# Turning the attention probabilities before they are split, with transfers between SBUF rows that complete the stacked operand

## The chip, the cores and the metric

One NeuronCore of a Trainium2 chip runs the whole program. It has five instruction streams of its own: TensorE (PE; its weight loads are shown as PEld), VectorE (DVE), ScalarE (ACT), GpSimd (POOL) and SyncE (SP). They wait for each other by semaphores only. SP and POOL mostly issue DMA transfers, and 16 DMA engines carry them. The metric is the device time of one execution in microseconds, the median of repeated runs.

## The reference

Sixteen batches of 512 rows by 512 columns go through an attention block against 77 context rows each, and then through a feed-forward block. Cut to what matters:

```
enc = layernorm(x);  dec = ctx                                  # 512 x 512 and 77 x 512, 16 batches
Sim = (enc @ w1)[:, :, None] + (dec @ w2)[:, None, :] + (enc * w3) @ dec^T + b_sim     # 512 x 77
A   = softmax(Sim over the 77);  hq_hat = A @ dec               # 512 x 512
hc  = sum_i softmax(max_j Sim)[i] * enc[i]                      # one row for each batch
x   = x + concat(enc, hq_hat, enc*hq_hat, enc*hc) @ W_qv + b_qv
h   = layernorm(x) @ W1 + b1                                    # 512 -> 2048
q   = h + phase * w_imag * sin(theta + 0.1 h) * 0.1
out = x + relu(q) @ W2 + b2                                     # 2048 -> 512
```

## The kernel before

Every large product is made with split operands. A float32 value v is written as v_hi (v rounded to float32r, the type TensorE reads in one pass) and v_lo = v - v_hi. A product is then three matmuls, hi*hi, hi*lo and lo*hi, in helper `three` (L533 to L539). Where the contraction is only over the 77 context rows, two matmuls do the work of three: helper `stacked` (L541 to L546) puts parts on top of each other along the 128 partitions. The stacked operand `at_s` has two halves. Half 0 holds the 77 rows of A^T (high part) and below them rows 0 to 50 of its low part. Half 1 holds the 77 high rows again and below them rows 51 to 76 of the low part, so it has 103 rows. JA is 51 and JB is 103.

The loop `body` runs over 16 feed-forward tiles f = 0 to 15 for batch b, and in the same loop the attention of the next batch n = b + 1 is prepared, piece by piece. So the attention of batch 0 stands alone in an opening (`attention_first`, roughly the first 90 us), and attentions 1 to 15 are woven into bodies 0 to 14. The order on each engine is written out by hand with tests on f (NA is 10). For the probabilities of batch n the stages are:

- f = 5: `row_exponentials` (ACT, L922), `max_exponentials` (ACT, L926) and `probabilities` (DVE, L1251 to L1257) leave the normalised probabilities in `prob`, 128 partitions by 4 row tiles by 77.
- f = 6: `prob_high` (ACT, L932 and L933) writes their high part twice to `split_prob`, a view of the buffer `prs`; `prob_low` (DVE, two instructions of L1084) writes the low parts beside it.
- f = 8: `prob_turn` (PE, L680 and L681) turns the split copy with eight transposes into both banks of the PSUM tile `mis`, after the hidden product of tile 8. `second_stack_out` (DVE, L1273) copies half 1 to `at_s`; `stack_out` (ACT, L938, at f = 9) copies half 0.
- f = 9: `hq_hat(n, 0)` (PE, L543 and L544) is the first reader of `at_s`. The rest of the attention's products follow at f = 10.

In the first body (b = 0) the weights are also split once and stored. For it SP loads raw tiles of W1 and W2 (L439, L431), ACT and DVE split them (L892, L884 and L1084) and POOL stores them (L1606, L1612). Later bodies load the stored tiles with POOL (L1552, L1558). In the first body SP also loads the rows of batch 2 at f = 8 (`x_load`, L367). DMA issues wait in the order of the engine that issues them.

Of the kernel before, what the change touches and what calls it, by code (L numbers as in the profile page):

```python
# [37 lines left out]
P = 128  # L38
# [12 lines left out]
def xattn_ffn(nc, x, ctx_rows, w_sim, b_sim, W_qv, b_qv, W1, b1, theta, w_real, w_imag, W2, b2, x_turned, out):  # L51
# [14 lines left out]
    NA = 10  # L66
# [21 lines left out]
    with ExitStack() as ctx:  # L88
# [6 lines left out]
        def sem(name):  # L95
            return ctx.enter_context(nc.semaphore(name))
# [34 lines left out]
        at_s = sb("at_s", [P, 2, R], F32R)  # L131
        assert 2 * J + JB == 4 * J - JA
        split_prob = prs[:].rearrange("p a b r -> p (a b r)")[:, 0:RT * (2 * J + JB)].rearrange(
            "p (t k) -> p t k", t=RT)

        split_high = [split_prob[:, :, 2 * k * J:(2 * k + 1) * J] for k in range(2)]
        e_bc = sb("e_bc", [P, R])
# [71 lines left out]
        ebc_done = sem("ebc_done"); erec_done = sem("erec_done"); at_done = sem("at_done")  # L209
        split_hi = sem("split_hi"); split_lo = sem("split_lo"); at_out = sem("at_out")  # L210
        hqh_done = sem("hqh_done"); full_done = sem("full_done")
# [149 lines left out]
        def _(sp):  # L361
# [47 lines left out]
            def ctx_load(n):  # L409
# [15 lines left out]
                stack_load(n, hqw_raw, hqw_tail, hqw_dram, ctx_in)  # L425

            def raw_tile_load(p):

                need(sp, w_lo, count_of(0, p) - 1)
                src = tile_source(p, False, w2_dram, [wqv_dram[2, :, c] for c in range(C)])  # L430
                sp.dma_start(w_raw[:, p % 2], src).then_inc(w_raw_in[p % 2], 16)  # L431
# [62 lines left out]
            def body(b, par, first, last):  # L494
                n, pn = b + 1, 1 - par
                for f in range(FT):
# [10 lines left out]
                    if last:  # L507
                        continue
                    if n + 1 == B:
                        continue  # L510
# [21 lines left out]
        def _(pe):  # L532
# [142 lines left out]
            def prob_turn(n):  # L675
                pe.wait_ge(split_lo, 2 * (n + 1))
                pe.wait_ge(ebc_done, n + 1)
                for t in range(RT):
                    rows = slice(t * P, (t + 1) * P)
                    pe.transpose(mis[:, 1, rows], split_prob[:, t, 0:P].bitcast(F32), ident[:])  # L680
                    tr = pe.transpose(mis[0:JB, 0, rows], split_prob[:, t, 2 * J:2 * J + JB].bitcast(F32), ident[:])  # L681
                tr.then_inc(at_done, 1)

            def hq_hat(n, c):
                if c == 0:
                    pe.wait_ge(at_out, 2 * (n + 1))
                    pe.wait_ge(hq_lo, 2 * (n + 1))
                if c >= 2:
                    pe.wait_ge(prt_done, C * n + c - 1)
                stacked(mis[:, c % 2], lambda k, a: hqs[0:k, a, c * P:(c + 1) * P], lambda k, a: at_s[0:k, a],  # L690
                        True, True, hqh_done)
# [75 lines left out]
            def body(b, par, first, last):  # L767
                n, pn = b + 1, 1 - par
                for f in range(FT):
# [4 lines left out]
                    if f == 5 and not last:  # L774
                        spread_max(n)
                    if f == 8 and not last:
                        prob_turn(n)
# [38 lines left out]
        def _(sc):  # L816
# [111 lines left out]

            def prob_high(n):

                sc.wait_ge(prob_done, n + 1)
                nc.scalar.copy(split_high[0], prob[:]).then_inc(split_hi, 1)  # L932
                nc.scalar.copy(split_high[1], prob[:]).then_inc(split_hi, 1)  # L933

            def stack_out(n):
                sc.wait_ge(at_done, n + 1)
                need(sc, att_done, RT * n)
                nc.scalar.copy(at_s[:, 0], mis[:, 1]).then_inc(at_out, 1)  # L938

# [16 lines left out]
            def attention_first():  # L956
# [19 lines left out]
                max_exponentials(0)  # L976
                prob_high(0)
                high_parts(5)
                stack_out(0)
                context_high(0)  # L980
                high_parts(6)
                high_parts(7)
# [26 lines left out]
            def body(b, par, first, last):  # L1009
                n, pn = b + 1, 1 - par  # L1010
                for f in range(FT):
# [4 lines left out]
                    if f == 5 and not last:  # L1016
                        row_exponentials(n)
                    if f == 6 and not last:
                        prob_high(n)
                    if f == NA - 1 and not last:  # L1020
                        stack_out(n)
                        w0_high(n, 0)
# [51 lines left out]
        def _(ve):  # L1074
# [188 lines left out]

            def prob_low(n):

                ve.wait_ge(split_hi, 2 * n + 2)
                low(split_prob[:, :, J:2 * J], prob[:], split_high[0]).then_inc(split_lo, 1)
                low(split_prob[:, :, 3 * J:2 * J + JB], prob[:, :, JA:J], split_high[0][:, :, JA:J]
                    ).then_inc(split_lo, 1)

            def second_stack_out(n):
                ve.wait_ge(at_done, n + 1)
                ve.tensor_copy(at_s[0:JB, 1], mis[0:JB, 0]).then_inc(at_out, 1)  # L1273

# [87 lines left out]
            def attention_first():  # L1362
# [28 lines left out]
                row_mean_scale(0)  # L1391
                prob_low(0)
                product_add(3)
                low_part(5)
                second_stack_out(0)
                row_mean(0)
# [39 lines left out]
            def body(b, par, first, last):  # L1436
                n, pn = b + 1, 1 - par
                for f in range(FT):
# [19 lines left out]
                    if f == NA - 2 and not last:  # L1458
                        second_stack_out(n)
                    if first and 3 <= f < 3 + CN - GAP:  # L1460
# [23 lines left out]
                    if f == 6 and not last:  # L1484
                        prob_low(n)
                        row_mean_scale(n)
                        row_mean(n, range(0, C // 2))
# [199 lines left out]
```

## Time and profile before

| | |
|---|---|
| median of 3 runs | 1985.26 us (1984.53 to 1986.4) |
| profiled execution, its own time | 1987.21 us |
| its span, first to last instruction | 1985.3 us |
| mean granted TensorE clock | 0.995 |
| PE busy | 1955.8 us, 99% |
| DVE busy | 1388.4 us, 70% |
| ACT busy | 980.0 us, 49% |
| period of one body, from any line to the same line one batch on | 119.1 us |

A group of rows gives a line of the kernel, the engine, the operation and what it writes and reads. A timeline row has start and duration in microseconds; what stands in brackets at its end is the idle time before it and what ended it. PE's rows overlap: a matmul of 512 columns is shown with 0.39 us, and the next starts 0.23 us after it, so the distance of the starts is what a matmul costs.

### The profile page before, as it was taken

Reading aid. Unit: us, or ns where it says so; the run is one execution under the profiler, and the core shown is the slowest. Engines: PE = TensorE matmul, PEld = TensorE weight load, DVE = VectorE, ACT = ScalarE, POOL = GpSimd, SP = SyncE. Lnnn points to the kernel's source line nnn. Section 1 sums busy time; section 2 is a strip of 40 time slices with the busy share of each in tenths; the row PEclk is TensorE's granted clock in tenths of the full one; section 3 lists DMA queues with packets and bytes.
Section 4 is the critical chain, followed back from the end, with each engine's and each line's share of the span. In section 5 each row is a group of like instructions: output and inputs, shape, how many; then the busy total and the mean of one; then the engine's idle time right before and its main releaser. Section 6 shows DMA issues by size and latency. Waiting matters only on the chain.

```text
span 1985.3 us, 24769 instructions
## 1 busy us (share of the span) xinstructions
PE 1955.8 (99%) x8832; PEld 1604.4 (81%) x8832; DVE 1388.4 (70%) x2406; ACT 980.0 (49%) x1654; POOL 385.5 (19%) x834
## 2 busy tenths in 40 slices
PE   6989999999999999999999999999999999999999
PEld 5777788888888888888888888888888888888887
DVE  6787776767767577676767767577676767767554
ACT  6474553635446363553635446363553635446343
POOL 0122212121121212112121121212112121121110
PEclk9999999999999999999999999999999999999999
DMA  7466947658476674748748476674748648475473
GB/s 256 153 227 233 303 148 239 216 158 242 148 220 196 195 226 145 233 148 240 216 159 242 147 221 196 193 227 145 232 148 239 217 161 239 146 223 184 140 216 122
DMA packets 142599, 394.17 MB, mean 199 GB/s; under 512 B 25655, under 2 KB 35379, under 8 KB 140556
## 3 DMA queue, kind: packets, MB, share of 16 engines
q0 software_dynamic: 83584, 304.31, 49.6%
q1 hardware_dynamic: 58748, 88.23, 14.2%
q8 instruction: 72, 1.18, 0.2%
q14 instruction: 51, 0.42, 0.1%
q10 hardware_dynamic: 144, 0.04, 0.0%
HBM read 351.68 MB, written 40.85 MB: 198 GB/s over the span
## 4 chain that ended last, share of the span: by engine, by line
PE 92%; DMA 2%; DVE 2%; ACT 1%; issue 1%; SPq 0%; ACTq 0%; POOL 0%; DVEq 0%; POOLq 0%
PE acc L535 17%; PE acc L537 17%; PE acc L536 17%; PE hid L535 12%; PE hid L537 11%; PE hid L536 11%; PE mis L636 1%; DMA w_raw<-in_L_ffn_W 1%; PE mis L543 1%; PE acc L544 1%; PE acc L543 1%; PE mis L544 1%; PE mis L537 1%; PE mis L535 1%; PE mis L536 1%
## 5 line engine op out<-in xcount | busy, mean ns | idle before, releaser
L535 PE MATMUL hid<-T,w1s 128*128 128x512 f32 x1024 | 404.9, 395 | 8.0 <-DVE w1s L1084 6.5
L535 PE MATMUL acc<-ws,act 128*128 128x512 f32 x1024 | 403.1, 394 | 0.0
L537 PE MATMUL hid<-T,w1s 128*128 128x512 f32 x1024 | 400.5, 391 | 0.0
L536 PE MATMUL hid<-T,w1s 128*128 128x512 f32 x1024 | 400.2, 391 | 0.0
L537 PE MATMUL acc<-ws,act 128*128 128x512 f32 x1024 | 399.9, 390 | 0.0
L536 PE MATMUL acc<-ws,act 128*128 128x512 f32 x1024 | 399.4, 390 | 0.0
L1224 DVE TENSOR_SCALAR kk<-ph 128x512 f32<-128x512 f32 x256 | 108.9, 425 | 353.1 <-ACT ph L899 353.1
L908 ACT ACTIVATE act<-h 128x512 fp32r<-128x512 f32 x256 | 162.0, 633 | 349.4 <-DVE h L1216 328.2
L899 ACT ACTIVATE ph<-hid,hbias 128x512 f32<-128x512 f32 x256 | 175.6, 686 | 306.3 <-PE hid L537 305.7
L1558 POOL DMA_DIRECT2D ws<-w2x_dram x240 | 127.1, 530 | 555.2 <-PE acc L537 545.7
L535 PEld LDWEIGHTS hid<-T,w1s 128*128 128x128 f32 x1024 | 193.4, 189 | 50.6 <-DVE w1s L1084 7.7
L1230 DVE SCALAR_TENSOR_TENSOR act<-h,act 128x512 fp32r<-128x512 f32 x256 | 176.1, 688 | 74.1 <-ACT act L908 72.8
L537 PEld LDWEIGHTS hid<-T,w1s 128*128 128x128 f32 x1024 | 193.1, 189 | 40.9
L537 PEld LDWEIGHTS acc<-ws,act 128*128 128x128 f32 x1024 | 192.6, 188 | 40.6
L536 PEld LDWEIGHTS hid<-T,w1s 128*128 128x128 f32 x1024 | 193.5, 189 | 38.9
L535 PEld LDWEIGHTS acc<-ws,act 128*128 128x128 f32 x1024 | 192.6, 188 | 39.3
L536 PEld LDWEIGHTS acc<-ws,act 128*128 128x128 f32 x1024 | 192.7, 188 | 38.9
L1552 POOL DMA_DIRECT2D w1s<-w1x_dram x240 | 128.9, 537 | 456.0 <-PE hid L537 444.0
L1216 DVE SCALAR_TENSOR_TENSOR h<-ph,camp,h 128x512 f32<-128x512 f32 x256 | 191.0, 746 | 0.0
L902 ACT ACTIVATE h<-hid,cols 128x512 f32<-128x512 f32 x256 | 174.2, 680 | 26.1 <-DVE act L1230 26.1
L1226 DVE TENSOR_TENSOR ph<-ph,kk 128x512 f32<-128x512 f32 x256 | 177.3, 693 | 8.8
L912 ACT ACTIVATE ph<-ph 128x512 f32<-128x512 f32 x256 | 158.3, 618 | 0.4
(181 smaller groups left out, 2739.3 us busy)
## 6 DMA issues: line engine op xcount, KB each, us to landing
w1s<-w1x_dram POOLq DMA_DIRECT2D x240, 512.0 KB, 3.8
ws<-w2x_dram POOLq DMA_DIRECT2D x240, 512.0 KB, 4.5
ws<-wqx_dram POOLq DMA_DIRECT2D x56, 512.0 KB, 3.6
full<-in_x_turned SPq DMA_DIRECT2D x15, 1024.0 KB, 8.1
out_x<-X SPq DMA_DIRECT2D x15, 1024.0 KB, 4.8
X<-in_x SPq DMA_DIRECT2D x14, 1024.0 KB, 6.7
w_raw<-in_L_ffn_W SPq DMA_DIRECT2D x32, 256.0 KB, 4.9
w1x_dram<-w1s POOLq DMA_DIRECT2D x16, 512.0 KB, 3.8
```

The costliest lines, as they stand in the source:

```text
L535: pe.matmul(dst, w_hi, m_hi, start=start, stop=False)
L536: pe.matmul(dst, w_hi, m_lo, start=False, stop=False)
L537: mm = pe.matmul(dst, w_lo, m_hi, start=False, stop=stop)
L899: nc.scalar.activation(ph[:, f % 2], hid[:, f % 2], ACT.Identity, bias=hbias[:, f:f + 1], scale=HSCALE).then_inc(t_done, 1)
L902: nc.scalar.activation(h2[:, f % 2], hid[:, f % 2], ACT.Identity, bias=b1c[:, f:f + 1], scale=1.0).then_inc(h2_done, 1)
L908: nc.scalar.activation(act[:, f % 4, 0], h2[:, f % 2], ACT.Relu).then_inc(act_hi, 1)
L912: nc.scalar.activation(ph[:, f % 2], ph[:, f % 2], ACT.Sin, scale=TWO_PI_BELOW).then_inc(s_done, 1)
L1216: ve.scalar_tensor_tensor(out=h2[:, f % 2], in0=ph[:, f % 2], scalar=camp[:, f:f + 1], in1=h2[:, f % 2], op0=ALU.mult, op1=ALU.add).then_i ...
L1226: ve.tensor_tensor(ph[:, f % 2], ph[:, f % 2], kk[:], ALU.subtract).then_inc(r_done, 1)
L1230: ve.scalar_tensor_tensor(out=act[:, f % 4, 1], in0=h2[:, f % 2], scalar=0.0, in1=act[:, f % 4, 0].bitcast(F32), op0=ALU.max, op1=ALU.subtract
L1552: po.dma_start(w1s[:, s].rearrange("p a c k -> p (a c k)"), w1x_dram[f % FT].rearrange("p a c k -> p (a c k)")).then_inc(w1_in[s], 16)
L1558: po.dma_start(ws[:, slot_of(p)], tile_source(p, last, w2x_dram, wqx_dram)).then_inc(w_in[slot_of(p)], 16)
```

## The change

The probabilities are no longer split before they are turned. PE turns `prob` itself with four transposes, at f = 7 in place of 8. ACT copies the turned 77 rows from PSUM into half 0 as their high part, and copies that from SBUF into half 1. DVE subtracts the high part from the PSUM rows and writes all 77 low rows to `at_lo`, a free piece of `prs` on partitions 0 to 76. Two DMA transfers then move the low rows to the partitions below the high ones, 51 rows of 2 KB into half 0 and 26 rows into half 1. SP issues them at f = 8, and ACT does so in the opening. `hq_hat(n, 0)` waits for both.

```
-        at_s = ...; split_prob = prs[...]; split_high = [...]
+        at_lo = prs[0:J, 1, 1]
...
+            def stack_low_in(n):                                    # SP, at f == NA - 2
+                sp.wait_ge(at_low, n + 1)
+                sp.dma_start(at_s[J:P, 0].bitcast(F32), at_lo[0:JA].bitcast(F32)).then_inc(at_in, 16)
+                sp.dma_start(at_s[J:JB, 1].bitcast(F32), at_lo[JA:J].bitcast(F32)).then_inc(at_in, 16)
...
             def prob_turn(n):
-                pe.wait_ge(split_lo, 2 * (n + 1))
-                pe.wait_ge(ebc_done, n + 1)
+                pe.wait_ge(prob_done, n + 1)
                 for t in range(RT):
-                    pe.transpose(mis[:, 1, rows], split_prob[:, t, 0:P].bitcast(F32), ident[:])
-                    tr = pe.transpose(mis[0:JB, 0, rows], split_prob[:, t, 2 * J:2 * J + JB].bitcast(F32), ident[:])
+                    tr = pe.transpose(mis[0:J, 1, t * P:(t + 1) * P], prob[:, t], ident[:])
...
             def hq_hat(n, c):
                 if c == 0:
+                    pe.wait_ge(ebc_done, n + 1)
                     pe.wait_ge(at_out, 2 * (n + 1))
+                    pe.wait_ge(at_in if n else at0_in, 32 * max(n, 1))
...
-            def prob_high(n): ...                                   # ACT, two copies, f == 6
             def stack_out(n):                                       # ACT, f == NA - 1 before, NA - 2 now
                 sc.wait_ge(at_done, n + 1)
-                nc.scalar.copy(at_s[:, 0], mis[:, 1]).then_inc(at_out, 1)
+                nc.scalar.copy(at_s[0:J, 0], mis[0:J, 1]).then_inc(at_out, 1)
+                sc.wait_ge(at_out, 2 * n + 1)
+                nc.scalar.copy(at_s[0:J, 1], at_s[0:J, 0].bitcast(F32)).then_inc(at_out, 1)
+            def first_stack_low_in(): ...                           # ACT, opening: the two transfers of batch 0
...
-            def prob_low(n): ...                                    # DVE, two subtractions, f == 6
-            def second_stack_out(n): ...                            # DVE, one copy, f == 8
+            def stack_low(n):                                       # DVE, f == 8
+                ve.wait_ge(at_out, 2 * n + 1)
+                low(at_lo, mis[0:J, 1], at_s[0:J, 0]).then_inc(at_low, 1)
```

On PE, in the first body, these rows stand between two matmul groups before the change (f = 8; the hidden product ends above, the product with W2 begins below):

```order
L680 MATMUL mis<-ident,prs 128x128 [waits ebc_done,split_lo]
L681 MATMUL mis<-ident,prs 103x128
L680 MATMUL mis<-ident,prs 128x128
L681 MATMUL mis<-ident,prs 103x128
L680 MATMUL mis<-ident,prs 128x128
L681 MATMUL mis<-ident,prs 103x128
L680 MATMUL mis<-ident,prs 128x128
L681 MATMUL mis<-ident,prs 103x128
```

And these stand there now, one tile earlier, with the matmuls on either side:

```order
L541 MATMUL hid<-T,w1s 128x512
L682 MATMUL mis<-ident,prob 77x128 [waits prob_done]
L682 MATMUL mis<-ident,prob 77x128 x3
L539 MATMUL acc<-ws,act 128x512 [waits w_lo,act_lo]
L540 MATMUL acc<-ws,act 128x512
```

Eight rows have become four, the wait is for the probabilities alone, and the place is after the hidden product of tile 7.

On SP, in the first body around f = 8, before the change (L431 loads raw tiles for the second weights, L439 those of W1, L367 the rows of batch 2):

```order
L439 DMA w_raw<-in_L_ffn_W 128x4x128 [waits w1_lo]
L431 DMA w_raw<-in_L_xattn_W_qv 128x512 [waits w_lo]
L367 DMA X<-in_x 128x4x512 [waits p_late2,p_late3,p_late1,p_late0]
L439 DMA w_raw<-in_L_ffn_W 128x4x128 [waits w1_lo]
L431 DMA w_raw<-in_L_xattn_W_qv 128x512 [waits w_lo]
```

The same place now (L426 and L427 are the new transfers, L363 and L441 the loads named before):

```order
L433 DMA w_raw<-in_L_xattn_W_qv 128x512 [waits w_lo]
L426 DMA at_s<-prs 51x512 [waits at_low]
L427 DMA at_s<-prs 26x512
L363 DMA X<-in_x 128x4x512 [waits p_late2,p_late3,p_late1,p_late0]
L441 DMA w_raw<-in_L_ffn_W 128x4x128 [waits w1_lo]
```

The load of batch 2 and the raw W1 tile now stand behind SP's wait for `at_low`.

On ACT, in the opening, before the change (L846 and L851 are the copies of the next context chunk):

```order
L938 CAST at_s<-mis 128x512 [waits at_done]
L876 CAST hqs<-ctx_raw 128x512 [waits hq0_in]
L877 CAST hqs<-ctx_raw 39x512
L876 CAST hqw<-ctx_raw 128x512 [waits hqw0_in]
L877 CAST hqw<-ctx_raw 39x512
L846 CAST act<-acc 128x504 [waits c_mm,c_tr]
```

And now:

```order
L935 CAST at_s<-mis 77x512 [waits at_done]
L937 CAST at_s<-at_s 77x512 [waits at_out]
L879 CAST hqs<-ctx_raw 128x512 [waits hq0_in]
L880 CAST hqs<-ctx_raw 39x512
L879 CAST hqw<-ctx_raw 128x512 [waits hqw0_in]
L880 CAST hqw<-ctx_raw 39x512
L942 DMA at_s<-prs 51x512 [waits at_low]
L943 DMA at_s<-prs 26x512
L849 CAST act<-acc 128x504 [waits c_mm,c_tr]
```

One copy and two DMA issues have come in ahead of the next context chunk.

## Rows read from the trace of the kernel before

**Rows 1.** The page: busy us, share of the span and instructions.
```profile
PE 1955.8 (99%) x8832; PEld 1604.4 (81%) x8832; DVE 1388.4 (70%) x2406; ACT 980.0 (49%) x1654; POOL 385.5 (19%) x834
```

**Rows 2.** Waits of PE: total us, times, longest.
```profile
PE hid L535 <- DVE w1s L1084: 6.5, 2, 3.6
...
PE mis L543 <- DVE hqw L1084: 2.7, 1, 2.7
```

**Rows 3.** Timeline of PE in a later body: start, duration.
```profile
983.49 0.39 PE L537 MATMUL hid<-T,w1s 128*128 128x512 f32 x1
983.72 0.27 PE L680 MATMUL mis<-ident,prs 128*128 128x128 f32 x1
...
984.83 0.40 PE L536 MATMUL acc<-ws,act 128*128 128x512 f32 x1
...
992.78 0.39 PE L543 MATMUL mis<-at_s,hqs 128*128 128x512 f32 x1
```

**Rows 4.** Timeline of DVE in that body.
```profile
977.41 0.65 DVE L1084 TENSOR_TENSOR prs<-prob,prs 128x308 fp32r<-128x308 f32 x2
...
980.72 0.43 DVE L1224 TENSOR_SCALAR kk<-ph 128x512 f32<-128x512 f32 x1 [0.54 <-ACT ph L899]
...
987.69 0.69 DVE L1273 CAST at_s<-mis 103x512 fp32r<-103x512 f32 x1
```

**Rows 5.** Timeline of ACT in that body.
```profile
974.27 0.44 ACT L932 CAST prs<-prob 128x308 fp32r<-128x308 f32 x1
...
974.96 0.69 ACT L899 ACTIVATE ph<-hid,hbias 128x512 f32<-128x512 f32 x1
```

**Rows 6.** Timeline of SP: a 6 KB store, the load that waits for it, a 51-row load.
```profile
1035.28 0.32 SPq L377 DMA_DIRECT2D stat_dram<-mean_bc  x1
1036.63 0.34 SPq L381 DMA_DIRECT2D mean_bc<-stat_dram  x1
...
1039.55 0.31 SPq L404 DMA_DIRECT2D ctx_raw<-in_ctx  x1
```

**Rows 7.** Windows: us, busy by engine, PEclk, share of the 16 DMA engines, GB/s.
```profile
990.00:990.50 0.50, 0.50 (x3) 0.39 (x3) 0.50 (x1) 0.25 (x1) 0.00 (x0) 1.00 1.10 410
...
1040.50:1040.75 0.25, 0.25 (x5) 0.25 (x4) 0.00 (x0) 0.25 (x1) 0.02 (x1) 1.00 0.19 59
```

**Rows 8.** The page: a kind of DMA issue, KB each, median us to landing.
```profile
w_raw<-in_L_ffn_W SPq DMA_DIRECT2D x32, 256.0 KB, 4.9
```

**Rows 9.** Timeline of POOL in that body, a weight load.
```profile
987.79 0.53 POOL L1558 DMA_DIRECT2D ws<-wqx_dram  x1 [3.08 <-PE acc L537]
```

**Rows 10.** Timeline of ACT, then DVE, then PE in the opening.
```profile
41.53 0.59 ACT L938 CAST at_s<-mis 128x512 fp32r<-128x512 f32 x1 [1.70 <-PE mis L681]
...
53.37 0.68 DVE L1084 TENSOR_TENSOR act<-acc,act 128x504 fp32r<-128x504 f32 x1 [0.51 <-ACT xin L851]
...
47.88 0.77 PE L543 MATMUL mis<-at_s,hqs 128*128 128x512 f32 x1 [2.65 <-DVE hqw L1084]
...
54.22 0.39 PE L543 MATMUL mis<-at_s,hqs 128*128 128x512 f32 x1
```

**Rows 11.** First body: SP, DVE, ACT and PE around the raw W1 tile.
```profile
147.02 0.38 SPq L367 DMA_DIRECT2D X<-in_x  x1
147.44 0.51 SPq L439 DMA_DIRECT2D w_raw<-in_L_ffn_W  x1
...
148.74 0.68 DVE L1273 CAST at_s<-mis 103x512 fp32r<-103x512 f32 x1
...
156.01 0.62 ACT L892 CAST w1s<-w_raw 128x512 fp32r<-128x512 f32 x1 [3.32 <-DMA w_raw<-in_L_ffn_W]
...
157.41 0.79 PE L535 MATMUL hid<-T,w1s 128*128 128x512 f32 x1 [2.88 <-DVE w1s L1084]
```

**Rows 12.** Windows: granted TensorE clock in the first body and after it.
```profile
157.41:163.10 5.69, 5.69 (x13) 4.46 (x14) 4.88 (x8) 1.34 (x3) 1.06 (x2) 0.50 0.84 285
...
1000.00:1900.00 900.00, 900.00 (x4088) 741.20 (x4087) 626.06 (x1073) 431.12 (x718) 179.87 (x392) 1.00 0.63 193
```

More of the change, by code:

```diff
@@ L131, in xattn_ffn @@
         at_s = sb("at_s", [P, 2, R], F32R)
[L132 to L136, printed above, removed]
+        at_lo = prs[0:J, 1, 1]
         e_bc = sb("e_bc", [P, R])
@@ L209, in xattn_ffn @@
         ebc_done = sem("ebc_done"); erec_done = sem("erec_done"); at_done = sem("at_done")
-        split_hi = sem("split_hi"); split_lo = sem("split_lo"); at_out = sem("at_out")
+        at_out = sem("at_out"); at_low = sem("at_low"); at_in = sem("at_in"); at0_in = sem("at0_in")
         hqh_done = sem("hqh_done"); full_done = sem("full_done")
@@ L508, in body @@
                         continue
+                    if f == NA - 2:
+                        stack_low_in(n)
                     if n + 1 == B:
@@ L675, in prob_turn @@
             def prob_turn(n):
-                pe.wait_ge(split_lo, 2 * (n + 1))
-                pe.wait_ge(ebc_done, n + 1)
+                pe.wait_ge(prob_done, n + 1)
                 for t in range(RT):
-                    rows = slice(t * P, (t + 1) * P)
-                    pe.transpose(mis[:, 1, rows], split_prob[:, t, 0:P].bitcast(F32), ident[:])
-                    tr = pe.transpose(mis[0:JB, 0, rows], split_prob[:, t, 2 * J:2 * J + JB].bitcast(F32), ident[:])
+                    tr = pe.transpose(mis[0:J, 1, t * P:(t + 1) * P], prob[:, t], ident[:])
                 tr.then_inc(at_done, 1)
@@ L775, in body @@
                         spread_max(n)
-                    if f == 8 and not last:
+                    if f == 7 and not last:
                         prob_turn(n)
@@ L927, in max_exponentials @@
                                      ).then_inc(ebc_done, 1)
[L929 to L933, printed above, removed]
             def stack_out(n):
@@ L937, in stack_out, with first_stack_low_in @@
                 need(sc, att_done, RT * n)
-                nc.scalar.copy(at_s[:, 0], mis[:, 1]).then_inc(at_out, 1)
+                nc.scalar.copy(at_s[0:J, 0], mis[0:J, 1]).then_inc(at_out, 1)
+                sc.wait_ge(at_out, 2 * n + 1)
+                nc.scalar.copy(at_s[0:J, 1], at_s[0:J, 0].bitcast(F32)).then_inc(at_out, 1)
+            def first_stack_low_in():
+                sc.wait_ge(at_low, 1)
+                nc.scalar.dma_start(at_s[J:P, 0].bitcast(F32), at_lo[0:JA].bitcast(F32)).then_inc(at0_in, 16)
+                nc.scalar.dma_start(at_s[J:JB, 1].bitcast(F32), at_lo[JA:J].bitcast(F32)).then_inc(at0_in, 16)
             def w0_high(n, c):
@@ L976, in attention_first @@
                 max_exponentials(0)
-                prob_high(0)
                 high_parts(5)
@@ L980, in attention_first @@
                 context_high(0)
+                first_stack_low_in()
                 high_parts(6)
@@ L1017, in body @@
                         row_exponentials(n)
-                    if f == 6 and not last:
-                        prob_high(n)
+                    if f == NA - 2 and not last:
+                        stack_out(n)
                     if f == NA - 1 and not last:
-                        stack_out(n)
                         w0_high(n, 0)
@@ L1262, in row_mean_scale @@
                 ve.reciprocal(erec[:], esum[:]).then_inc(erec_done, 1)
[L1264 to L1273, printed above, removed]
+            def stack_low(n):
+                ve.wait_ge(at_out, 2 * n + 1)
+                low(at_lo, mis[0:J, 1], at_s[0:J, 0]).then_inc(at_low, 1)
             def row_mean(n, chunks=range(C)):
@@ L1391, in attention_first @@
                 row_mean_scale(0)
-                prob_low(0)
                 product_add(3)
                 low_part(5)
-                second_stack_out(0)
+                stack_low(0)
                 row_mean(0)
@@ L1458, in body @@
                     if f == NA - 2 and not last:
-                        second_stack_out(n)
+                        stack_low(n)
                     if first and 3 <= f < 3 + CN - GAP:
@@ L1484, in body @@
                     if f == 6 and not last:
-                        prob_low(n)
                         row_mean_scale(n)
```

## The prediction

> **What bounds the kernel now.** I read the page first. PE is busy 99% of the span, DVE 70% and ACT 49% [rows 1]. The reader should see that no other engine can be the bound over the whole program. Next come PE's waits. They are few: the longest two groups are 6.5 us in two waits on a raw W1 tile and 2.7 us in one wait in the opening [rows 2]. Then PE's timeline. The last wait of more than a few tenths ends at 157.41 [rows 11], and from 1000 to 1900 PE is busy 900.00 of 900.00 us at full clock [rows 12]. So the program has two parts. In the opening and in body 0 the chain runs through ACT, DVE, SP and DMA as well as PE, and PE stalls. In bodies 1 to 14 time is what PE issues, and an instruction there that goes is a gain, as long as no new wait takes its place. Last come the timelines of DVE, ACT, SP and POOL around the places the change touches.
>
> **Transposes in bodies 1 to 14.** The eight transposes start at 983.72, and the second matmul after them starts at 984.83 [rows 3]. That is 1.11 us, less the 0.23 us of the one matmul between, so 0.88 us for eight, 0.11 us each. (The 0.27 us shown for one overlaps its neighbours; multiplying it by the count would claim too much.) The four that remain have the same 128 moving columns and fewer stationary ones, so I take 0.11 us for them too. The saving is 0.44 us in a body and 14 x 0.44 = 6.2 us. Moved to f = 7 they start about 978.3, and their only wait, for the probabilities, is long met: ACT already copies those at 974.27 [rows 5]. So the new place costs nothing.
>
> **ACT and DVE in a body.** ACT loses two copies at f = 6, 0.69 us by the distance from 974.27 to 974.96 [rows 5], and gains one of about 0.57 us, now ahead of the phase of tile 8. That phase waits for PE's hidden product anyway, which comes 0.44 us later relative to the transposes. DVE loses 0.57 us at 977.41, and has one 0.69 us instruction for another at 987.69 [rows 4]. Neither bounds a later body, so I count 0. What this does set is when the low rows are ready. DVE waited at 980.72 for ACT [rows 4], and that ACT work comes 0.69 us earlier. DVE is full from there, so the low rows start near 987.0 and end near 987.7.
>
> **The new wait in bodies 1 to 14.** `hq_hat` starts at 992.78 now [rows 3] and would start at 992.34. The transfers have 4.6 us. Their landing is not in the trace, so I bound it. A 6 KB store and the load that waits for it are issued 1.35 us apart [rows 6]; this is the fixed part under load. The 51 rows are 104 KB. In the window in which a 51-row load is likely to be alone, 0.19 of the 16 engines, about three, carry 59 GB/s [rows 6, 7], which makes 1.8 us. A weight load of 512 KB shares these engines. POOL issues it at 987.79 [rows 9], 0.44 us earlier after the change. Its 32 KB on each engine, at 410/16 = 26 GB/s [rows 7], make 1.3 us. The sum is 4.4 us, so landing is near 992.1, and the cover is 0.2 us. The low end spreads 104 KB over all engines at 410 GB/s, 0.3 us, so 1.6 us in all and a cover of 3.0. The high end is the 4.9 us in which 256 KB land behind other loads [rows 8], plus 0.35 us for the second issue: 5.3 us, a wait of 0.7 us, 9.8 us over 14 bodies. I take 0, near the middle value, knowing that the cover is thin.
>
> The window shows about three busy engines. The Trainium skill has a rule for it (DMA: Bandwidth & Descriptors, section "Why a DMA increments its semaphore by 16 and not by 1"): the number of engines is the largest one up to 16 that divides the row count. By that rule 51 rows run on 3 engines and 26 on 13, which speaks against cutting the stack at 51; the trace agrees with its 0.19. Without the rule the low end would be the likely one.
>
> Queued behind SP's wait for `at_low` there is nothing near in a later body: the rows of the next batch are loaded before it, the turned rows 25 us after it.
>
> **The opening: +0.8 us.** ACT copies the stack at 41.53, when PE's transposes end [rows 10]. With four fewer this is near 41.1. Then it makes two copies with a wait between (1.2 us) in place of one, which puts the next work 0.25 us later. Two DMA issues follow, 0.31 us each in SP's row [rows 6] and more with the gaps, 0.75 us in all. So the next context chunks come 1.0 us later, and ACT has nothing idle before the last of them: DVE waits for ACT at 53.37 [rows 10]. DVE would end this one near 55.0 in place of 54.05. PE starts its next stacked product at 54.22 [rows 10], so it would start near 55.0. The 0.44 us of the transposes vanish in the wait that ends at 47.88 [rows 10]. The transfers are issued near 44.9 and land near 48, as the wait for `hqw` ends. Bounds: 0.3 if the issues are short, 1.3 if the landing at 48 slips too.
>
> **Body 0: +1.8 us.** PE stalls 2.88 us until 157.41 for the raw W1 tile of f = 11. SP issued that load at 147.44 behind the 1 MB load at 147.02, and ACT got it at 156.01 [rows 11]. Now both stand behind `at_low`. DVE reaches that place at 148.74 [rows 11], 0.7 us sooner after the change because the f = 6 pieces are off this body's chain, so the low rows are ready near 148.7. Two issues of 0.35 us and one of 0.4 us put the raw W1 load at 149.9, 2.4 us later. The landing should move less, since the 1 MB cannot start before the tile load ahead of it is through, and one such load takes 4.9 us [rows 8]. Half of 2.4 is 1.2 us, the rows of the stack in front add up to 0.7 us. I take 1.8, between 1.2 and 2.6. The 0.44 us of the transposes are lost in this stall, and so is the wait for the stack transfers just ahead of it.
>
> **The clock: -0.5 us.** After the stall the granted clock is 0.50 for 5.69 us [rows 12], which is the 1.2 GHz level, and costs about 2.8 us. The stall of the opening has the same after it. A later restart may find a shorter slow stretch, or a longer one elsewhere. I bound this by -2.8 and +2.8 and take a small gain, because PE would restart closer to the end of the present stretch.
>
> **Sum.** -6.2 + 0.8 + 1.8 - 0.5 = -4.1 us. The profiled execution took 1987.21 us and would take 1983.1. The median is 1.95 us below that execution, 1985.26, so the prediction is 1981.2 us.
>
> **Rivals.**
> 1. *The transfers land late and PE waits in each body.* One mechanism: the transfer of 51 rows on few engines beside a weight load. From 0.29 us a body it eats the whole net gain, and at the high end of 0.7 us the time is 1981.2 + 9.8 = 1991.0, slower. For it: the cover of 0.2 us, and the 4.9 us of a loaded queue [rows 8]. Against it: the 1.35 us round trip [rows 6] and the sum of 4.4. The Trainium skill (same page, section "Latency and other measured facts") has a fixed cost of about 2 us, most of it the receipt from the target, with HBM the slowest. With it in place of 1.35 the landing would be 5.1 us and the wait 0.5; the trace's own round trip, written to HBM, is shorter.
> 2. *The early part eats the gain.* Opening 1.3, body 0 2.4, and 1.5 us more at the slow clock: -6.2 + 5.2 = -1.0, so 1984.3 us. For it: ACT and DVE are full where the pieces are added [rows 10]. Against it: it needs all three at their upper ends.
> 3. *Body 0 gets shorter.* The removed split lay on its chain, 0.69 us of ACT and 0.57 us of DVE [rows 4, 5], and the slow stretch may go. Opening 0.5, body 0 0.6, clock -2.8: -7.9, so 1977.4 us. Against it: SP's order, which does not depend on these.
>
> That the transposes are not really halved is excluded by the order of PE's instructions.
>
> **How the numbers follow.** The forecast (cover holds) has 0.52, with its own range 1978.5 to 1984; rival 1 has 0.20, rival 2 0.14, rival 3 0.14. A measurement of this kernel tells about 0.2%, 4.0 us, from no change, so the line is at 1981.3 and the forecast lies on it: 0.31 of it counts as faster and 0.21 as the same. Rival 3 and a little of rival 2 make faster 0.47. Same is 0.21 + 0.03 (a short wait of rival 1) + 0.11 = 0.35. Slower is 0.17 + 0.01 = 0.18. The range runs from below rival 3 to rival 1's full wait: 1977.0 to 1991.0.
>
> **What would show it.** PE's four transposes at a distance of 0.11 us, and a body of 118.7 us in place of 119.1. No idle time before the first `at_s` matmul in bodies 1 to 14; a wait there for `at_s` by DMA shows rival 1. In the opening the matmul of 54.22 near 55.0. In body 0 the stall before the hidden product of f = 11 ending near 160 in place of 157.41, with SP's raw W1 issue near 150. The prediction is wrong if the body is not shorter, or if the first 165 us grow by more than 4 us or shrink.

## The result and the profile after: slower by 0.6%

| | before | after |
|---|---|---|
| median | 1985.83 us (1984.53 to 1986.93, 4 runs) | 1999.39 us (1996.83 to 2000.4, 4 runs) |
| ratio | | 1.0061, 95% interval [1.0048, 1.0073] |
| span of the profiled execution | 1985.3 us | 1998.6 us |
| period of a body | 119.12 us | 119.83 us |

The prediction said 1981.2 us, and 1991.0 at most. The time went the other way and beyond the range, and the body, which was to be 118.7 us, is longer than before.

The page of the changed kernel, busy us, share and instructions (before: [rows 1]):

```profile
PE 1949.5 (98%) x8768; PEld 1594.1 (80%) x8768; DVE 1378.9 (69%) x2374; ACT 980.5 (49%) x1638; POOL 385.7 (19%) x834
```

PE has 64 instructions fewer and is busy 6.3 us less, as intended, and the span is still 13.3 us longer. So PE must wait somewhere new. Its waits (total us, times, longest; before: [rows 2]) name the place:

```profile
PE mis L547 <- DMA at_s<-prs: 17.2, 15, 4.0
...
PE hid L539 <- DMA w1s<-w1x_dram: 2.5, 1, 2.5
PE mis L640 <- DVE xin L1331: 2.2, 1, 2.2
```

Fifteen waits for the transfers, one in each body from 0 to 14. None of them was there before. PE's timeline in the body that [rows 3] shows:

```profile
985.50 0.39 PE L541 MATMUL hid<-T,w1s 128*128 128x512 f32 x1
985.72 0.60 PE L682 MATMUL mis<-ident,prob 128*77 128x128 f32 x4
986.08 0.48 PE L539 MATMUL acc<-ws,act 128*128 128x512 f32 x1
...
999.56 0.39 PE L541 MATMUL acc<-ws,act 128*128 128x512 f32 x1
1000.63 0.47 PE L547 MATMUL mis<-at_s,hqs 128*128 128x512 f32 x1 [0.68 <-DMA at_s<-prs]
1000.94 0.40 PE L548 MATMUL mis<-at_s,hqs 103*128 103x512 f32 x1
```

The four transposes take 0.44 us where eight took 0.88, counted as in the prediction: the second matmul behind them starts at 986.39, so 0.67 us less the 0.23 of one matmul. The first matmul on `at_s` was due at 999.79, 0.23 us after the one before it, and starts at 1000.63. That is 0.84 us late. The bracket says 0.68, since it counts from the shown end of a matmul that overlaps the next. In the 14 later bodies the bracket is between 0.66 and 1.22 us, 0.94 on average, which makes 1.10 us of lateness.

Windows of PE show both sides of it: between 1000 and 1900 PE was busy 900.00 us [rows 12] and now is idle for 7.5 us of the same stretch, eight waits in eight bodies:

```profile
1000.00:1900.00 900.00, 892.46 (x4032) 732.73 (x4033) 622.16 (x1059) 428.74 (x708) 177.77 (x388) 1.00 0.63 192
```

**The chain in front of that matmul.** DVE, ACT, SP and POOL in the same body (before: [rows 4 to 6], [rows 9]):

```profile
994.43 0.68 DVE L1088 TENSOR_TENSOR prs<-mis,at_s 77x512 fp32r<-77x512 f32 x1
...
990.37 0.56 ACT L935 CAST at_s<-mis 77x512 fp32r<-77x512 f32 x1
990.97 0.62 ACT L937 CAST at_s<-at_s 77x512 fp32r<-77x512 f32 x1
...
995.14 0.79 SPq L426 DMA_DIRECT2D at_s<-prs  x1
995.98 0.87 SPq L427 DMA_DIRECT2D at_s<-prs  x1
...
994.81 0.53 POOL L1553 DMA_DIRECT2D ws<-wqx_dram  x1 [2.19 <-PE acc L541]
```

The reader should see three things. DVE's input, ACT's first copy, was ready at 990.93 (990.37 + 0.56), and the subtraction started 3.5 us later, since DVE's order puts it behind the sine term of tile 8. Each issue holds SP for 0.8 us and not the 0.31 of a 51-row load from memory [rows 6]. And POOL issued 512 KB of weights 0.33 us before the first transfer. The windows after that (share of the 16 engines and GB/s are the last two columns) show what moved:

```profile
995.50:996.00 0.50, 0.50 (x4) 0.42 (x3) 0.50 (x2) 0.40 (x2) 0.00 (x0) 1.00 0.00 0
996.00:997.00 1.00, 1.00 (x6) 0.84 (x5) 0.91 (x2) 0.43 (x1) 0.00 (x0) 1.00 0.87 209
997.00:998.00 1.00, 1.00 (x7) 0.81 (x6) 0.17 (x2) 0.73 (x2) 0.47 (x1) 1.00 0.93 328
```

Two microseconds of all engines, about the 512 KB of the weight load, come first. The list of DMA packets (queue, packets, MB, share of the 16 engines; POOL's transfers go through q0, those of SP through q1) has the stack's rows apart. From 995.14 to 997.90, and then from 997.90 to 999.70:

```profile
q0 software_dynamic: 136, 0.51, 62.2%
```

```profile
q0 software_dynamic: 50, 0.17, 45.1%
q1 hardware_dynamic: 93, 0.16, 25.4%
```

All 77 rows of the stack lie in the second stretch. So the first row moves 2.76 us after the issue, the last one is through 1.79 us later, and PE starts 0.94 us after that, together 5.49 us. PE was due 4.65 us after the issue. In the 14 later bodies the first row moves 2.56 to 2.87 us after the issue, and PE starts 5.42 to 6.02 us after it, 5.74 on average.

**Body 0.** SP and then PE (before: [rows 11]):

```profile
146.74 0.83 SPq L426 DMA_DIRECT2D at_s<-prs  x1
147.62 0.84 SPq L427 DMA_DIRECT2D at_s<-prs  x1
...
149.94 0.80 SPq L441 DMA_DIRECT2D w_raw<-in_L_ffn_W  x1
...
152.11 0.77 PE L547 MATMUL mis<-at_s,hqs 128*128 128x512 f32 x1 [4.01 <-DMA at_s<-prs]
159.51 0.50 PE L539 MATMUL hid<-T,w1s 128*128 128x512 f32 x1 [1.43 <-DVE w1s L1088]
...
212.63 1.11 PE L640 MATMUL mis<-ident,xin 128*128 128x128 f32 x8 [2.15 <-DVE xin L1331]
227.65 0.50 PE L539 MATMUL hid<-T,w1s 128*128 128x512 f32 x1 [2.53 <-DMA w1s<-w1x_dram]
```

The raw W1 load goes out at 149.94 (147.44 before), and the stall behind it ends at 159.51 (157.41 before). Two later waits for what the raw tiles feed are new or longer.

Where the 13.3 us of the two profiled executions lie: up to the last wait of the opening (117.61 before, 116.61 now) the changed kernel is 1.0 us ahead. From there to the start of `hq_hat(2, 0)` in body 1 it loses 5.0 us. The 13 periods from there to body 14 cost 9.2 us, and the end 0.1.

### The profile page after: what moved, and what is told of

Read it like the earlier page. It is cut to its first block, busy times and chain, and to the rows that moved or that the text cites. A ratio compares the mean times of both kernels' runs of the same rounds, so it can differ in the third digit from the quotient of the medians.

```text
span 1998.6 us, 24625 instructions
## 1 busy us (share of the span) xinstructions
PE 1949.5 (98%) x8768; PEld 1594.1 (80%) x8768; DVE 1378.9 (69%) x2374; ACT 980.5 (49%) x1638; POOL 385.7 (19%) x834
## 3 DMA queue, kind: packets, MB, share of 16 engines
q8 instruction: 71, 1.16, 0.2%
## 4 chain that ended last, share of the span: by engine, by line
PE 72%; DVE 9%; ACT 7%; DMA 6%; issue 5%; SPq 1%; POOL 0%; ACTq 0%; DVEq 0%; POOLq 0%
PE acc L539 13%; PE acc L541 13%; PE acc L540 13%; PE hid L539 9%; PE hid L541 9%; PE hid L540 9%; DMA at_s<-prs 3%; DVE h L1220 2%; ACT L915 2%; ACT ph L902 2%; DVE kk L1228 1%; PE mis L640 1%; ACT L929 1%; DVE ph L1230 1%; DMA w_raw<-in_L_ffn_W 1%
```

## The experiments

All times are compared with the kernel before on the same chip. "Late" is the longest bracket before the first `at_s` matmul in bodies 1 to 14. "Early part" is the start of `hq_hat(2, 0)`, which stands in body 1, less the start of the last transposes that wait in the opening (117.61 before, 116.61 after). This mark itself lies between 116.4 and 118.6 us in the eleven profiles, so what comes before it is left out. The early part is that of one profile for each kernel and moves too; the ratio rests on all the timed runs.

| run | ratio and interval | period, us | late, us | early part, us |
|---|---|---|---|---|
| before | 1 | 119.12 | none | 160.45 |
| after | 1.0061 [1.0048, 1.0073] | 119.83 | 1.22 | 165.44 |
| a_no_transfers | 0.9967 [0.9955, 0.998] | 118.65 | none | 158.87 |
| b_rows_45_32 | 1.0007 [0.9998, 1.0016] | 118.86 | 1.20 | 165.15 |
| c_low_earlier | 0.9985 [0.9976, 0.9993] | 118.65 | none | 163.49 |
| d_first_body_order | 1.0068 [1.0056, 1.0081] | 119.68 | 1.16 | 163.89 |
| i_small_load_ahead | 0.9985 [0.9976, 0.9994] | 118.67 | none | 164.02 |
| e_early_51 | 0.9975 [0.9965, 0.9985] | 118.65 | none | 160.76 |
| f_early_45 | 0.9971 [0.9961, 0.9982] | 118.59 | none | 159.72 |
| g_low_earlier_45 | 0.998 [0.9971, 0.9989] | 118.59 | none | 160.09 |
| h_body0_none | 0.9971 [0.9962, 0.9979] | 118.65 | none | 162.55 |

**1. The price of the wait.** SP issues no transfer in the bodies, and PE waits for none.

```diff
-                    if f == NA - 2:
-                        stack_low_in(n)
-                    pe.wait_ge(at_in if n else at0_in, 32 * max(n, 1))
+                    pe.wait_ge(at0_in, 32)
```

> Leaves out the two transfers in bodies 0 to 14, so the low rows that stand in at_s are those of batch 0; all else is the changed kernel. Theory (the landing of the transfers costs each of the 14 later bodies 0.94 us of waiting and some 0.2 us of restart): the period falls from 119.83 to 118.68 us, PE shows no wait before the first at_s matmul, and body 0 loses SP's two issues of 0.83 us; 1999.4 - 16 - 1 to 4 = 1979 to 1983 us, below the kernel before. Rival 1 (the period is longer because of the new order of PE, ACT and DVE, and the wait only takes up slack that is there anyway): the period stays above 119.3 and the time above 1990. Rival 2 (only the early part is hurt by the transfers): period 119.8, time 1996.

Measured: 1980.17 us against 1987.48, ratio 0.9967, period 118.65. PE's timeline:

```profile
987.16 0.40 PE L539 MATMUL acc<-ws,act 128*128 128x512 f32 x1
987.40 0.39 PE L545 MATMUL mis<-at_s,hqs 128*128 128x512 f32 x1
```

No bracket: the wait is gone, and the body is 1.17 us shorter than in the changed kernel and 0.47 us shorter than before. The theory holds, and both rivals fall. 0.94 us of idle time cost 1.17: 0.16 for the overlap that the bracket leaves out, and the rest in the first matmuls behind the wait (0.31 us apart in place of 0.23). The last is argued from the rows, not tested. The 0.47 us is what the body gains by the transposes and the new order together, and 14 times it, 6.6 us, is all of this kernel's lead over the kernel before by the ratio (0.33%, 6.6 us).

**2. Fewer rows on more engines.** The cut of the low rows is moved from 51 and 26 to 45 and 32.

```diff
-    JA = P - J
+    JA = 45
```

(`P` becomes `J + JA` where half 0 is filled and multiplied.)

> The changed kernel with the stack cut at 45 and 32 low rows in place of 51 and 26 (halves of 122 and 109 rows). The Trainium skill (DMA: Bandwidth & Descriptors, section Why a DMA increments its semaphore by 16 and not by 1) has the number of engines as the largest up to 16 that divides the row count: 15 and 16 here, in place of 3 and 13. Theory A (the 51 rows on three engines are what makes the landing late; 17 rows each one after the other, the packets run 1.75 us): the packets take about 0.5 us, the wait of 0.94 us in a body goes, period 118.7, time near 1984. Theory B (the wait is the issue on SP of 0.8 us twice, and the queue behind the weight load that POOL issues 0.33 us earlier): the landing is at most 0.3 us earlier, period 119.5 or more, time 1995 to 1999.

Measured: ratio 1.0007, period 118.86, 0.96 us shorter than in the changed kernel. SP's issues take nearly as long as before (0.90 and 0.60 us, together 1.50 in place of 1.66), and the weight load is as near. SP and POOL in its timeline:

```profile
991.01 0.90 SPq L426 DMA_DIRECT2D at_s<-prs  x1
991.96 0.60 SPq L427 DMA_DIRECT2D at_s<-prs  x1
...
990.67 0.53 POOL L1553 DMA_DIRECT2D ws<-wqx_dram  x1 [2.19 <-PE acc L541]
```

From 991.01 to 993.60 only q0 moves packets. From 993.60 to 994.80:

```profile
q1 hardware_dynamic: 108, 0.16, 39.9%
```

The first row moves 2.61 us after the issue, as late as before, but the last one is through 1.05 us later, in place of 1.79. So the three engines of the 51 rows cost about 0.9 us of landing in this body (3.66 us to the end of the last row in place of 4.55) and 0.96 of the period. The Trainium skill's rule that the number of engines is the largest one up to 16 that divides the row count (DMA: Bandwidth & Descriptors, section "Why a DMA increments its semaphore by 16 and not by 1") forecasts 15 and 16 here, and this run agrees: besides the 77 rows, q1 has 31 short packets here and 16 in the changed kernel, that is 15 + 16 and 3 + 13. Three of the 14 bodies still show a wait (1.20, 0.59 and 0.24 us), and the period is 0.27 us above the 118.59 of the kernels below with the same cut and no wait, so the cover is about nothing here. Theory A's 1984 us was too low, and so was its 0.5 us for the packets. Theory B fails: the period is below its 119.5.

**3. The same transfers 2.3 us sooner.** Only the place of DVE's subtraction moves.

```diff
-                    if f == NA - 2 and not last:
-                        stack_low(n)
...
                     if f == 7 and not last:
                         row_mean(n, range(C // 2, C))
                         context_low(n)
+                        stack_low(n)
```

> The changed kernel with DVE's subtraction of the stack at the end of tile 7 instead of after the sine term of tile 8, where its input has been ready for 2.9 us. Theory (only the lateness counts): the low rows are ready 2.3 us sooner, the landing is before PE gets to the first at_s matmul, the period is 118.7 and the time 1999.4 - 16 = 1983.5 or less. Rival 1 (the transfers always run right behind the next weight load, whose issues are 2.72 us apart, so that moving them 2.3 us moves the landing by less than 1 us or not at all): period 119.4 to 119.8, time 1994 to 1999. Rival 2 (DVE has no 0.6 us to give there and the product with W2 waits for act): period above 119.3 with waits of PE for act.

Measured: ratio 0.9985, period 118.65, no wait in the later bodies. The theory holds (1984.3 us, where 1983.5 or less was expected). DVE had the 0.68 us of this instruction to give: PE shows no new wait for it. From the first issue to the matmul it is now 6.97 us. The wait in body 0 stays, 2.92 us in place of 4.01.

**4. The load ahead.** This separates the queue from the issue and the engines. The weight load issued just ahead of the transfers is cut to an eighth.

```diff
-                po.dma_start(ws[:, slot_of(p)], tile_source(p, last, w2x_dram, wqx_dram)
+                q = 16 if p == FIRST + C - 1 and not last else P
+                po.dma_start(ws[0:q, slot_of(p)], tile_source(p, last, w2x_dram, wqx_dram)[0:q]
```

> The changed kernel with one weight load of each later body cut down: the load that POOL issues 0.33 us before the two transfers of the stack (994.81 against 995.14 in the changed kernel) brings 16 partitions, 64 KB, in place of 128, 512 KB; the other 112 partitions keep older weights. Theory (the transfers start only when that load is through, 2.7 us after their issue, of which 1.8 us is the queue): they start and land 1 to 1.8 us sooner, the wait of 0.94 us before the first at_s matmul goes or falls under 0.1, period 118.65 to 118.75, ratio 0.998 to 0.999. Rival (the time goes in SP's issues of 0.8 us, the three engines and the receipt, and the load ahead has no part): the wait stays above 0.6 us, period 119.5 or more, ratio 1.004 or above.

Measured: ratio 0.9985, period 118.67, no wait above 0.1 us in the later bodies. POOL and SP, then a window:

```profile
988.89 0.51 POOL L1554 DMA_DIRECT2D ws<-wqx_dram  x1 [2.19 <-PE acc L541]
...
989.24 0.79 SPq L426 DMA_DIRECT2D at_s<-prs  x1
```

```profile
990.50:991.50 1.00, 1.00 (x6) 0.84 (x5) 0.69 (x1) 0.17 (x2) 0.00 (x0) 1.00 0.17 37
```

The packets from 989.24 to 990.66, and then from 990.66 to 992.93:

```profile
q0 software_dynamic: 40, 0.07, 23.2%
```

```profile
q1 hardware_dynamic: 93, 0.16, 23.3%
```

With nothing large ahead the first row moves 1.43 us after the issue, in place of 2.76 (1.38 to 1.44 in the 14 later bodies). At 0.17 of 16, about three engines, one sees the 51 rows alone. The last row is through 3.68 us after the issue, in place of 4.55. So the weight load ahead held the start back by 1.33 us and the landing by 0.87 of the 5.49 us (0.97 in the mean of the 14 bodies); why the rows take longer from first to last when they start sooner (2.26 us against 1.79) was not tested. The theory holds against its rival. The cover is about nothing here too: 3.68 and the 0.94 us from the last row to PE make 4.62, and PE is due at 4.65.

**5. Body 0, SP's order.** The rows of batch 2 and the raw W1 tile go first.

```diff
                             raw_w1_load(f + 2)
+                        if f == NA - 1:
+                            stack_low_in(n)
-                    if f == NA - 2:
+                    if f == NA - 2 and not first:
```

> The changed kernel with SP's order in body 0 alone changed: the load of batch 2's rows and the raw W1 tile of f = 11 first, the two transfers of the stack behind them. Theory (the early part is 4.0 us longer since these loads stand behind the transfers in SP's order): the stall before the hidden product of f = 11 ends near 157.5 again, as in the kernel before, the first at_s matmul of body 0 waits longer, and the start of hq_hat(2,0) is 2 to 4 us sooner than 282.05; time 1995.5 to 1997.5. Rival (what is longer is set by ACT and DVE behind the first at_s matmul of body 0): the early part is as long or longer, time 1999 to 2002. The period stays at 119.83 by both.

Measured: ratio 1.0068, 1999.75 us, not distinguishable from the changed kernel. Neither text had it whole: by the time the rival is right, and in the profile the early part is 1.6 us shorter. The raw W1 load did go out at 145.00, as meant. But the transfers stood behind the 1 MB load, and PE waited 8.96 us for them:

```profile
147.01 0.84 SPq L426 DMA_DIRECT2D at_s<-prs  x1
...
157.33 0.76 PE L549 MATMUL mis<-at_s,hqs 128*128 128x512 f32 x1 [8.96 <-DMA at_s<-prs]
```

154 KB took 10.3 us from issue to use. So with either order one of the two groups is late in body 0, as long as the low rows are ready only at 147.

**6. Body 0 without its two transfers,** otherwise as in 3.

```diff
-                    if f == NA - 2:
+                    if f == NA - 2 and not first:
                         stack_low_in(n)
```

> As c_low_earlier, but body 0 leaves out its two transfers, so that batch 1 is computed with the low rows of batch 0; bodies 1 to 14 have theirs. Theory (the transfers of body 0 alone cost 4.6 us there by SP's order and the wait behind them): the early part, hq_hat(2,0) less the start of body 0, falls from 163.5 to 159, time near 1980.5 where the kernel before has 1987.5, ratio 0.9965. Rival (the early part depends on chance in the opening, 1 us either way, more than on the transfers): ratio 0.998 or above.

Measured: ratio 0.9971 against 0.9985 for number 3. The difference, 0.0014 or 2.8 us, is the best estimate of what body 0's transfers cost there, though the intervals of the two just overlap. The ratio speaks for the theory (0.9965) and against the rival, whose 0.998 lies just outside the interval. But the early part of the profiled execution, 162.55, did not fall to 159 as expected. In it the raw W1 tile, issued at 147.35, reached ACT at 157.56, 10.2 us later, where it took 9.0 in a_no_transfers. One profile is not enough to size this part, so its size rests on the timed runs.

**7. All of it earlier.** The transposes at f = 6, ACT's copies and DVE's subtraction at the start of f = 7, and in body 0 the transfers between the raw W1 tile of f = 10 and the next raw tile, once with 51 rows, once with 45.

```diff
-                    if f == 7 and not last:
+                    if f == 6 and not last:
                         prob_turn(n)
-                    if f == NA - 2 and not last:          # ACT stack_out, DVE stack_low
+                    if f == NA - 3 and not last:
```

> The changed kernel with the whole chain one tile earlier: PE's four transposes at f = 6, ACT's two copies and DVE's subtraction at the start of f = 7, and in body 0 SP issues the two transfers between the raw W1 tile of f = 10 and the next raw tile, not behind that tile. Theory (in body 0 SP has nothing to do but wait for the low rows from 144.3 on, and everything it issues later pays for that): the raw W1 load of f = 11 goes out near 146 instead of 149.9, the first at_s matmul of body 0 waits under 1 us, hq_hat(2,0) starts near 277 to 279 instead of 282.05, the period is 118.65: 1981 to 1983 where the kernel before has 1987.5 (ratio 0.9965 to 0.998). Rival (the early subtraction on DVE and the copies on ACT delay the sines in body 0, which is full there, by as much as they give): hq_hat(2,0) at 281 or later, ratio 0.9985 or above.

> The same chain one tile earlier, and the stack cut at 45 and 32 rows. Theory: in later bodies nothing is left to gain, period 118.65; in body 0 the transfers are 1 us shorter, which counts only if the first at_s matmul still waits there: ratio equal to that of the same kernel with 51 rows, or up to 0.0005 below it. Rival (fewer engines per transfer leave room for the raw tile loads beside them, so that 15 and 16 engines hold those up): 0.0005 above it.

Measured: 0.9975 and 0.9971. Both lie in the range that was expected for the first (0.9965 to 0.998), and with 51 rows `hq_hat(2, 0)` starts at 277.93, as the theory had it. With 45 rows the time is 1981.2 us against 1987.48, faster than the kernel before by 0.29% and than the changed one. SP in body 0 of the kernel with 45 rows, then PE:

```profile
140.76 0.96 SPq L426 DMA_DIRECT2D at_s<-prs  x1
141.76 0.62 SPq L427 DMA_DIRECT2D at_s<-prs  x1
...
145.40 0.38 SPq L363 DMA_DIRECT2D X<-in_x  x1
145.83 0.51 SPq L441 DMA_DIRECT2D w_raw<-in_L_ffn_W  x1
...
156.39 0.80 PE L541 MATMUL hid<-T,w1s 128*128 128x512 f32 x1 [4.68 <-DVE w1s L1090]
```

The transfers now fill time in which SP had nothing to issue, the raw load is out at 145.83 in place of 149.94, and the first `at_s` matmul of body 0 has no wait. The early part is 159.72, 5.7 us shorter than in the changed kernel, of which about 1.2 is body 1's own wait. The two cuts differ by less than their intervals.

**8. The earlier subtraction and 45 rows.** The edits of 3 and 2 together.

> The subtraction at the end of tile 7 (as in the run named c_low_earlier) and the cut at 45 and 32. Theory: period 118.65 as there; in body 0 the wait of 2.9 us before the first at_s matmul becomes about 1.9, the early part is up to 1 us shorter: ratio 0.998 to 0.9985. If 0.9985 is missed on the upper side, the length of the transfers has no part in body 0.

Measured: 0.998, as expected but not distinguishable from 0.9985. The wait of body 0 is 1.26 us in place of 2.92 (1.9 was expected), and from the first issue to the matmul it is 4.59 us in place of 6.84. So the engines seem to have a part there too; it is one profile of each.

## Why the prediction was wrong

**The step that failed** is "The new wait in bodies 1 to 14": a landing of 4.4 us, a cover of 0.2 us, "I take 0". Its cover was right (4.64 us forecast, 4.68 measured from the end of the subtraction to PE's due time). The landing took 5.49 in the body shown and 5.74 on average. By the parts of the sum, in the body shown:

| part | forecast | measured |
|---|---|---|
| all that is fixed | 1.35 us | 2.37 us: 1.43 from the issue to the first row with nothing large ahead (number 4), and 0.94 from the last row to PE's matmul |
| the rows of the stack on three engines | 1.8 us | 1.79 us, first to last row |
| the weight load ahead | 1.3 us | 1.33 us later start (2.76 in place of 1.43) |
| sum | 4.4 us | 5.49 us |

The fixed part was the term that was mis-sized, by 1.0 us, and the other two were right to a tenth. (The measured parts add up by construction, since the load's part is the difference of two starts.) The forecast's 1.35 came from a 6 KB store and the load that waits for it, 1.35 us apart [rows 6], whose issue is short (0.32 us against 0.79). The Trainium skill has about 2 us (DMA: Bandwidth & Descriptors, section "Latency and other measured facts"), which I cited and set aside in favour of the trace's shorter pair. The measured 2.37, which includes PE's start, is nearer to it, though HBM, which it names as the slowest target, has no part in these transfers. That two terms came out exactly is in part luck: one was read from a window that was only likely to hold the load alone, and the weight load's 1.33 us at the start is worth only 0.87 at the landing.

It was a mistake of judgement too. A cover of 0.2 us on a sum of three bounded terms is a coin toss with 14 bodies behind it, and it got a chance of 0.52 against 0.20. Rival 1 was the mechanism, and the high end of its landing, 5.3 us, was near. Its price was low, 0.7 us a body against 1.17: the landing is later still, so PE is 1.10 us late on average, and the restart adds 0.08. So the later bodies cost 9.9 us where a gain of 6.2 was forecast, and this alone takes the time out of the range.

**The transposes** were right: 0.44 us a body forecast, 0.44 by their starts and 0.47 by the period (number 1). Moving them to f = 7 cost nothing that shows.

**The later bodies' sum.** 14 x (1.17 - 0.47) = 9.8 us longer by the price of the wait, 9.9 by the periods, 14 x (119.83 - 119.12).

**The opening** was forecast as 0.8 us longer and is not: PE starts its next stacked product at 53.09, where 54.22 was before [rows 10] and 55.0 the forecast. ACT in the opening:

```profile
39.88 0.58 ACT L935 CAST at_s<-mis 77x512 fp32r<-77x512 f32 x1 [2.11 <-PE mis L682]
40.49 0.62 ACT L937 CAST at_s<-at_s 77x512 fp32r<-77x512 f32 x1
41.02 0.62 ACT L879 CAST hqs<-ctx_raw 128x512 fp32r<-128x512 f32 x1
41.21 0.83 ACTq L942 DMA_DIRECT2D at_s<-prs  x1
41.66 0.62 ACT L880 CAST hqs<-ctx_raw 39x512 fp32r<-39x512 f32 x1
42.07 0.83 ACTq L943 DMA_DIRECT2D at_s<-prs  x1
...
43.59 0.58 ACT L849 CAST act<-acc 128x504 fp32r<-128x504 f32 x1
```

The same chunk before:

```profile
44.60 0.58 ACT L846 CAST act<-acc 128x504 fp32r<-128x504 f32 x1
```

The two issues run beside the copies and add nothing between them. The added copy puts the next chunk 3.71 us behind the stack copy (3.07 before, 41.53 to 44.60), and the 0.44 us of the transposes pay for two thirds of it. The rest of the 1.0 us by which the opening is shorter is not explained by these rows. The clock, below, fits it, but the mark moves by as much from profile to profile.

**Body 0** was near in its landmarks: the raw W1 issue near 150 (149.94) and the stall's end near 160 (159.51). The 1.8 us was too small. From the mark in the opening the part is 5.0 us longer, of which about 1.2 is body 1's own wait, and the transposes hide 0.5 more, so body 0 lost about 4.3 in this profile. The medians, 13.6 us apart, less the 9.9 of the later bodies leave 3.7 us for opening and body 0 together, where 2.6 was forecast. The forecast stopped at the raw tile. It did not follow the later raw tiles, behind which `xin` and the stored W1 tiles are late (212.63 and 227.65). It also compared with the SP of before, which issued the 1 MB load at 147.02. In a_no_transfers that load goes out at 144.31, and in the changed kernel SP does nothing from 144.15 to 146.74 but wait for the low rows. So there may have been room in body 0 for rival 3's gain, which the transfers took: the early part of a_no_transfers is 1.6 us shorter than before, in one profile.

**The clock** had -0.5 us. The slow stretch of body 0 is still there, at 0.50, the 1.2 GHz level, and stands behind the wait for the stack:

```profile
150.67:157.50 6.83, 5.39 (x13) 4.26 (x14) 0.83 (x2) 0.00 (x0) 0.00 (x0) 0.50 1.03 342
```

Nothing here isolates its share. Over the first 90 us the granted clock is 0.96 before and 0.98 now (over the next 75 us 0.91 in both), so the opening got back up to 0.02 x 90 = 1.8 us of PE's time:

```profile
0.00:90.00 90.00, 74.39 (x335) 58.23 (x336) 60.61 (x127) 47.16 (x100) 10.21 (x28) 0.96 0.64 204
0.00:90.00 90.00, 73.10 (x335) 57.08 (x336) 60.90 (x125) 47.63 (x100) 10.21 (x28) 0.98 0.64 209
```

The forecast had the sign and its bounds right, but gave its reason at body 0, where the slow stretch did not shrink. That is luck.

## What to carry to other kernels

When a compute step is traded for a transfer, add up its landing from the moment the data is ready (the issue, the load that was issued just ahead, the rows per engine, the time from the last row to the reader's start), and where the cover is within a microsecond of that sum, take the wait as the likely case. The first cure is an earlier place in the order, here 0.68 us of DVE work moved by 2.3 us, which was worth 0.76%. A wait in the order of the issuing engine delays all that it issues later, so transfers belong where that engine is idle anyway.

## What the runs showed of the hardware

- Issuing the 51-row and 26-row transfers between SBUF rows held SP for 0.79 and 0.87 us. A 51-row load from memory took 0.31 in the kernel before [rows 6].
- On ACT such an issue lasts 0.83 us too, but ACT's copies went on beside it.
- A transfer issued 0.33 us behind a 512 KB weight load from another engine's queue moved nothing for 2.56 to 2.87 us, until that load was all but through. With 64 KB in its place the first row moved after 1.38 to 1.44 us.
- Between the last row of the stack and the matmul that waited for it, 0.94 to 1.18 us passed in the 14 later bodies.
- 51 and 26 rows left 16 short packets beside the 77 rows, 45 and 32 rows left 31, and from first to last row the two pairs took 1.79 and 1.05 us.
- With the cut at 45 and 32 rows, so 122 and 109 in place of 128 and 103, a body is 0.06 us shorter (118.59 against 118.65, in both pairs of kernels). The cause was not looked for.
